# Writing two stages of an attention and expert kernel out in straight code, with the expert tiles inside attention's block

## The chip, the cores and the metric

The kernel runs on one NeuronCore of one Trainium2 chip. The metric is the device time of one execution in microseconds (us), as the median of three runs. One further execution was recorded by the hardware profiler; all rows below are of that one. Engines are named as in the profile: PE (matrix engine; PEld is its weight load), DVE (vector), ACT (scalar), POOL (GpSimd) and SP (whose queue issues most DMAs).

## The reference

The input is x, 8 sequences of 512 tokens with 128 features. All arithmetic is float32.

```
xn = layernorm(x)
s  = attention(xn)         # theta = 0.5 + 0.2 sigmoid(qk) + 0.15 tanh(qk) + 0.1 relu(qk);
                           # softmax(theta) @ v, then the output projection
nf = layernorm(xn) * ln_w + ln_b
e, w = argmax(nf @ router), sigmoid(max(nf @ router))          # one of 8 experts per token
routed = (silu((w nf) @ gate[e]) * ((w nf) @ up[e])) @ down[e]
shared = (silu(nf @ sh_gate) * (nf @ sh_up)) @ sh_down
x  = x + s * silu(xn + routed + shared)
xn = layernorm(x)
x  = x + mamba(xn) * silu(quantised_ffn(xn))                   # state space scan of 16 states
```

## The kernel before, in words

A tile is 128 tokens on 128 partitions; a sequence is 4 tiles (TPB), all tokens are 32 tiles (NT). The kernel is hand written: each engine's program is a list in order, and semaphores join them. It stands in blocks; at a block's end every engine waits for the others.

1. First stage. Moments of all tokens are taken by DVE from `x_all`; then a hardware loop (`Fori`) over the 8 sequences. In each pass DVE makes the normed rows `xn_w` (L307) and twice normed rows `z_w` (L314), and from them `nf_all` (L320, L323). PE turns both (L247, L252), ACT copies them out of PSUM (L213, L217, L220), PE multiplies the turned rows with the value weights (L257) and the router (L263), and DVE writes `vo_all` and `logits` (L328, L333). POOL copies `xn_w` to `res_all` and `xnT_w` to `xnT_all` (L231, L233).
2. Routing. Top, one-hot, counts and the slot of each token, a chain of small DVE instructions (L391 to L434). Tokens are sorted by expert into 40 slot tiles (NT + 8), each of one expert. `guoff` holds each slot tile's expert.
3. Attention, a loop over sequences. Beside it POOL scales rows by their score into `xs_w` (L479) and scatters them to DRAM (`xs_dram`, L486), four indirect DMAs for a sequence.
4. Expert stage, 10 rounds of 4 slot tiles (8 of them in a `Fori`). For tile u: SP loads `xs_t`; PE turns it (`turn_x`, L797); ACT copies it (`x_out`, L864); PE multiplies it with gate and up (`up`, L809); ACT makes a tanh (`tanh`, L869); DVE makes `ha` and `hm` (`hidden`, L888 and L892); PE turns `hm` (`turn_h`, L816); DVE copies it (`h_out`, L898); PE multiplies with down (`dn`, L826); DVE copies the result (`y_out`, L905); SP stores it to `ys_dram` (L778). These are software pipelined over two buffers: in step u PE does `up(u + 1)`, `turn_x(u + 2)`, `dn(u - 1)`, `turn_h(u)`. The expert's number comes into a PE register by `value_load` from `guoff` (`load_expert`, L802, shown by the order as TENSOR_LOAD); the registers don't outlive a pass of the loop, so it is read again:

```
def steps(r, first, last):
    expert.clear()
    load_expert(r, 1)
    if not first:
        load_expert(r, -1)
    for u in range(UN):
        ...                     # up(u + 1), turn_x(u + 2)
        if u == 1:
            load_expert(r, 0)
        ...                     # dn(u - 1), then load_expert(u + 2) for u < 3, turn_h(u)
```

5. Gathering of the expert results, the gate, the second norm. 6. The scan and the quantised network, over half of the time. Stages 5 and 6 are not touched.

Of the kernel before, what the change touches and what calls it, by code (L numbers as in the profile page):

```python
# [5 lines left out]
def attention_moe_mamba_ffn(nc, t, out):  # L6
# [36 lines left out]
    with ctx:  # L43
# [45 lines left out]
        gu = sb("gu", [P, NE, 2 * I])  # L89
        down = sb("down", [P, NE, KI, D])  # L90
# [36 lines left out]
        logits = sb("logits", [P, NT, NE])  # L127
# [14 lines left out]
        with ExitStack() as ph:  # L142
            def sb1(name, shape, dt=fp32):
                return ph.enter_context(nc.sbuf_tensor(name, shape, dt))
            var = sb1("var", [P, NT])
            tmp = sb1("tmp", [P, NT])
            std = sb1("std", [P, NT])
            xn_w = sb1("xn_w", [P, TPB, D])
            z_w = sb1("z_w", [P, TPB, D])
            zw_w = sb1("zw_w", [P, TPB, D])  # L150
            xnT_w = sb1("xnT_w", [P, L])
            nfT_w = sb1("nfT_w", [P, L])
            zeros = sb1("zeros", [P, SLOT_TILES * D // 4])
            bvb = sb1("bvb", [P, P])
            names = {"xn_done": 1, "z_done": 1, "xT_ps": 1, "zT_ps": 1, "xnT_w_done": 1, "nfT_w_done": 1,
                     "vo_ps": 1, "logit_ps": 1, "vo_done": 1, "logit_done": 1, "xnT_copied": 1,
                     "xn_copied": 1, "nfT_copied": 1, "zw": 1, "nf": 1}
            S = {n: sem("p1_" + n) for n in names}
            s_dve = sem("p1_dve_step")
            s_var = sem("p1_var_ready")  # L160
            s_std = sem("p1_std_ready")
            s_zero = sem("p1_zeros_ready")
            s_zd = sem("p1_slots_zeroed")
            s_bvb = sem("p1_bv_broadcast")
            s_wvo = sem("p1_wvo_ps")
            s_wvo_sb = sem("p1_wvo_sb")

            def at(b, n, c=1):
                return (b + 1) * names[n] + c

            block = ph.enter_context(nc.Block())

            @block.sync
            def _(sp):
# [5 lines left out]
                for dst, src in [(WqT[:, :], t["WqT"]), (WkT[:, :], t["WkT"]),  # L180
                                 (shgu[:, 0:I], t["sh_gate"]), (shgu[:, I:2 * I], t["sh_up"]),
                                 (shdown[:, :, :], t["sh_down"].rearrange("(k p) h -> p k h", p=P)),
                                 (gu[:, :, 0:I], t["gate"].rearrange("e h i -> h e i")),
                                 (gu[:, :, I:2 * I], t["up"].rearrange("e h i -> h e i")),
                                 (down[:, :, :, :], t["down"].rearrange("e (k p) h -> p e k h", p=P))]:
# [6 lines left out]
                sp.wait_ge(s_zd, 64)  # L192

            @block.scalar
            def _(act):
# [6 lines left out]
                for dst, src in loads:  # L202
                    act.dma_start(dst, src).then_inc(s_w, 16)
                act.wait_ge(s_var, 1)
                nc.scalar.activation(std[:, :], var[:, :], ACT.Sqrt).then_inc(s_std, 1)
                act.wait_ge(s_var, 2)
                nc.scalar.activation(tmp[:, :], var[:, :], ACT.Sqrt).then_inc(s_std, 1)
                act.wait_ge(s_w, 16 * 12)
                with act.Fori(0, NB) as b:
                    act.wait_ge(S["xT_ps"], at(b, "xT_ps"))  # L210
                    act.wait_ge(S["vo_ps"], at(b, "vo_ps", 0))
                    act.wait_ge(S["xnT_copied"], at(b, "xnT_copied", 0))
                    nc.scalar.activation(xnT_w[:, :], bank[0], ACT.Copy).then_inc(S["xnT_w_done"], 1)  # L213
                    act.wait_ge(S["zT_ps"], at(b, "zT_ps"))
                    act.wait_ge(S["logit_ps"], at(b, "logit_ps", 0))
                    act.wait_ge(S["nfT_copied"], at(b, "nfT_copied", 0))
                    nc.scalar.activation(nfT_w[:, :], bank[1], ACT.Identity, bias=cols[:, 3:4],  # L217
                                         scale=cols[:, 2:3]).then_inc(S["nfT_w_done"], 1)
                    act.wait_ge(S["nfT_w_done"], at(b, "nfT_w_done"))
                    nc.scalar.activation(nfT_all[:, ds(b * L, L)], nfT_w[:, :], ACT.Copy).then_inc(S["nfT_copied"], 1)  # L220

            @block.gpsimd
            def _(pool):
# [3 lines left out]
                for n, per in names.items():  # L227
                    pool.sem_inc(S[n], per)
# [1461 lines left out]
```

## Time and profile before

| what | value |
|---|---|
| median of 3 runs | 908.47 us (906.34 to 909.36) |
| profiled execution: its time | 903.81 us |
| profiled execution: its span, first to last instruction | 901.5 us |
| PE, DVE, ACT, POOL busy, share of the span | 77%, 78%, 52%, 58% |
| first stage and routing | 0 to about 77 us |
| attention | about 77 to 230 us |
| expert stage | about 230 to 342 us |
| gathering, second norm, scan | about 342 to 901.5 us |

A row of the timeline is: start in us, duration in us, engine, line of the kernel, operation, out<-in with shapes, how many instructions were merged, and in brackets how long the engine had been idle before and what released it ("issue": nothing that the profile shows). A row of groups is: line, engine, operation, out<-in, count | busy us, mean ns of one | idle us before them. A row of windows is: stretch, its length, busy us (and instructions) of PE, PEld, DVE, ACT and POOL, granted clock of PE as a share of full speed, busy share of the DMA engines, GB/s.

### The profile page before, as it was taken

To read this page: it belongs to the slowest core of one execution; us is meant where nothing else is said; L and a number is where in the kernel's file an instruction comes from. 1 tells how busy PE (TensorE), PEld (TensorE's weight loads), DVE (VectorE), ACT (ScalarE), POOL (GpSimd) and SP (SyncE) were. 2 spreads that over 40 slices of the span, in tenths; PEclk is the share of its full clock that TensorE was granted. 3 is DMA by queue.
4 is the path that set the end of the run, shared out by engine and by line. 5 is a ranking of instruction groups with operands and counts; after the bars stand their busy time and mean duration, and the time that the engine had idled before them with its cause. 6 is when DMAs were issued, how large, how long until landed. Compare 5 with 4: busy or idle time off the path is not lost. (4 is left out here: it accounts for less than half of the span.)

```text
span 901.5 us, 14653 instructions
## 1 busy us (share of the span) xinstructions
PE 689.7 (77%) x3968; PEld 507.1 (56%) x3969; DVE 702.3 (78%) x1262; ACT 471.3 (52%) x874; POOL 521.4 (58%) x318
## 2 busy tenths in 40 slices
PE   1884999998777772107677988978889798997764
PEld 0771566556344441103346777766777676786763
DVE  5975687877355554881269999998999999999995
ACT  0431666665122221332568586785867869587451
POOL 0213671000000005730478999999899999999993
PEclk9966999999799996556999999999999999999899
DMA  8400110000211111100521142230322204131000
GB/s 233 165 0 15 33 35 12 0 0 0 74 47 50 52 47 35 44 20 1 187 95 54 42 131 71 46 133 25 130 70 65 111 26 150 49 107 71 25 12 12
DMA packets 40046, 55.79 MB, mean 62 GB/s; under 512 B 6584, under 2 KB 29632, under 8 KB 40000
## 3 DMA queue, kind: packets, MB, share of 16 engines
q1 hardware_dynamic: 36224, 50.48, 16.8%
q0 software_dynamic: 2048, 4.20, 1.6%
q10 hardware_dynamic: 1728, 0.57, 0.3%
q8 instruction: 19, 0.31, 0.1%
q14 instruction: 27, 0.22, 0.1%
HBM read 45.54 MB, written 9.70 MB: 61 GB/s over the span
## 5 line engine op out<-in xcount | busy, mean ns | idle before, releaser
L1585 DVE TENSOR_TENSOR_SCAN xnT_all<-psum,nfT_all 128x1024 f32<-128x1024 f32 x128 | 285.6, 2273 | 7.6 <-ACT psum L1435 4.7
L1323 PEld LDWEIGHTS psum<-W_out,xnT_all 128*128 128x128 f32 x2048 | 241.0, 195 | 37.1 <-issue 35.2
L1323 PE MATMUL psum<-W_out,xnT_all 128*128 128x128 f32 x2048 | 243.9, 278 | 16.4 <-DVE acc L1601 16.4
L1435 ACT ACTIVATE psum<-delta,A 128x511 f32<-128x511 f32 x256 | 163.2, 678 | 41.9 <-DVE xnT_all L1585 41.1
L1303 POOL TENSOR_TENSOR nfT_all<-nf_all,du 128x1024 f32<-128x1024 f32 x64 | 149.9, 2367 | 5.1 <-DVE xnT_all L1585 5.1
L1303 POOL TENSOR_TENSOR nfT_all<-attn_all,du 128x1024 f32<-128x1024 f32 x64 | 149.3, 2361 | 1.4 <-POOL du L1280 0.9
L960 POOL COPY pos_w<-pos 128x4 uint32 x8 | 1.6, 198 | 202.7 <-issue 202.5
L1601 DVE SCALAR_TENSOR_TENSOR acc<-psum,Cc,acc 128x128 f32<-128x128 f32 x352 | 96.7, 342 | 7.8 <-PE psum L1323 7.8
L1323 PE MATMUL psum<-vo_all,wgu 128*128 128x512 f32 (+1 forms) x96 | 46.7, 608 | 31.2 <-DVE hff L1621 29.6
L1323 PE MATMUL psum<-vo_all,W_taps 128*128 (+4 forms) x128 | 60.1, 617 | 1.7 <-DVE psum L1568 1.7
L809 PE MATMUL psum<-gu,xT 128*128 x80 | 46.6, 668 | 15.6 <-DVE hm L892 13.5
L864 ACT ACTIVATE xT<-psum 128x128 f32<-128x128 f32 x40 | 11.1, 278 | 80.4 <-PE psum L797 80.4
L981 PE MATMUL psum<-const,xn 128*128 128x128 f32 x32 | 8.3, 434 | 52.7 <-issue 31.5
L1260 POOL TENSOR_TENSOR lg<-lg,rl 128x1024 f32<-128x1024 f32 x8 | 18.8, 2347 | 49.8 <-ACT lg L1501 49.8
L536 PEld LDWEIGHTS psum<-vo_all,PT 128*128 128x128 f32 x256 | 31.8, 195 | 24.1 <-ACT PT L614 16.3
L1323 PEld LDWEIGHTS psum<-vo_all,wgu 128*128 128x128 f32 x96 | 16.3, 189 | 47.6 <-issue 29.4
L964 POOL DMA_INDIRECT moe_w<-ys_dram,pos_w x32 | 33.7, 1053 | 13.9 <-issue 8.9
L1456 ACT ACTIVATE ts<-psum,Cc 128x128 f32<-128x128 f32 x128 | 35.8, 357 | 10.1 <-PE psum L1323 10.1
L486 POOL DMA_INDIRECT xs_dram<-xs_w,pos_w x32 | 32.4, 1012 | 14.7 <-issue 9.9
L1323 PEld LDWEIGHTS psum<-vo_all,W_taps 128*128 128x128 f32 x128 | 24.3, 199 | 27.7 <-issue 25.6
L905 DVE COPY yt<-psum 128x128 f32<-128x128 f32 x40 | 11.7, 292 | 35.5 <-PE psum L826 35.5
L536 PE MATMUL psum<-vo_all,PT 128*128 (+1 forms) x256 | 38.0, 293 | 1.7 <-ACT PT L614 1.4
(202 smaller groups left out, 1261.4 us busy)
## 6 DMA issues: line engine op xcount, KB each, us to landing
attn_all<-bt_dram SPq DMA_DIRECT2D x32, 512.0 KB, 5.4
nf_all<-bt_dram SPq DMA_DIRECT2D x32, 512.0 KB, 3.6
xs_dram<-zeros SPq DMA_DIRECT2D x4, 640.0 KB, 7.3
xs_t<-xs_dram SPq DMA_DIRECT2D x40, 64.0 KB, 1.8
ys_dram<-yt SPq DMA_DIRECT2D x40, 64.0 KB, 1.6
x_all<-in_x_dram SPq DMA_DIRECT2D x8, 256.0 KB, 6.7
out_dram<-ow SPq DMA_DIRECT2D x8, 256.0 KB, 2.3
gu<-in_gate_dram SPq DMA_DIRECT2D x1, 1024.0 KB, 5.9
```

Of the source, the lines that this page charges most:

```text
L486: pool.indirect_dma_start(xs_dram, bass.IndirectOffsetOnAxis(ap=pos_w[:, i, j:j + 1], axis=0), xs_w[:, i, j, :], None).then_inc(s_sc[i], 16)
L536: ins = nc.tensor.matmul(bank[4][:, j * P:(j + 1) * P], PT[:, j % 2, c, :], vo_all[:, ds(b * TPB + c, 1), :], start=(c == 0), stop=(c == T ...
L809: nc.tensor.matmul(bank[2 + u % 2], xT[:, u % 2, :], gu_flat[:, ds(e * (2 * I), 2 * I)], start=True, stop=True).then_inc(S["gu_ps"], 1)
L905: nc.vector.tensor_copy(yt[:, u % UN, :], bank[6 + u % 2][:, 0:D]).then_inc(S["y"], 1)
L964: pool.indirect_dma_start(moe_w[:, i, j, :], None, ys_dram, bass.IndirectOffsetOnAxis(ap=pos_w[:, i, j:j + 1], axis=0)).then_inc(s_moe[i], 16)
L1260: nc.gpsimd.tensor_tensor(lg[:, :, :], lg[:, :, :], rl[:, :, :], ALU.add).then_inc(S["sp"], 1)
L1303: nc.gpsimd.tensor_tensor(dbx[:, i % R, :, :], B_pair(q), du[:, p, h:h + 1, :].to_broadcast([P, 2, L]), ALU.mult)\
L1323: return nc.tensor.matmul(o, l, r, start=start, stop=stop)
L1435: ins = nc.scalar.activation(dA[:, i % RA, k, 1:L], delta[:, p, h, 1:L], ACT.Exp, scale=A[:, h, 2 * q + k:2 * q + k + 1])
L1456: ins = nc.scalar.activation(ts[:, i, j, :], bank[Gb[n % 2]][:, j * P:(j + 1) * P], ACT.Copy, scale=Cc[:, p, j, n:n + 1])
L1585: nc.vector.tensor_tensor_scan(hring[:, i % R, :, :].rearrange("p n l -> p (n l)"), dA[:, i % RA, :, :].rearrange("p n l -> p (n l)"), dbx ...
L1601: nc.vector.scalar_tensor_tensor(acc[:, p, j, :], bank[Gb[m % 2]][:, j * P:(j + 1) * P], Cc[:, p, j, m:m + 1], acc[:, p, j, :] if i else s ...
```

## The change

First stage and routing become one block and are written out over the 8 sequences, with no loop. The norms are written straight to `res_all` and the turned rows to `xnT_all` and `nfT_all`, so the copies by POOL and by ACT (L220) are gone. `nf_all` is no longer made on DVE: PE turns `nfT_all` back (`turn_back`), and ACT writes it multiplied by the score (`scaled`); attention's POOL multiplies no more. The moments' chain is shorter, and the first norm starts before the second variance is known. Logits stay in PSUM, and DVE takes each sequence's top from there.

The scatters read `pos` and `nf_all` directly, and POOL waits after each four. The expert stage stands in attention's block: no block end between them, its buffers lie over `xnT_all`, and SP loads the first four slot tiles once the last keys have been multiplied. It is written out over the 40 tiles. Gate, up and down lie in one tensor `gud`, with one offset for an expert (its number times `WE`), read once for each tile. `y_out` has moved from DVE to ACT.

```
-            names = {"xn_done": 1, "z_done": 1, ...
-                with act.Fori(0, NB) as b:
...
-                    nc.scalar.activation(nfT_all[:, ds(b * L, L)], nfT_w[:, :], ACT.Copy).then_inc(S["nfT_copied"], 1)
-                with pool.Fori(0, NB) as b:
...
-                    nc.gpsimd.tensor_copy(res_all[:, ds(b * TPB, TPB), :], xn_w[:, :, :]).then_inc(S["xn_copied"], 1)
...
-                    nc.gpsimd.tensor_copy(xnT_all[:, ds(b * L, L)], xnT_w[:, :]).then_inc(S["xnT_copied"], 1)
+                def turn_back(b):
+                    if b >= 2:
+                        pe.wait_ge(S["xs"], b + 1 - 2)
+                    for i in tiles(b):
+                        ins = nc.tensor.transpose(bank[bN[b % 2]][:, cols4(i)], nfT_all[:, i * P:(i + 1) * P], ident)
+                    ins.then_inc(S["nf_ps"], 1)
...
+                for b in range(NB + 1):
+                    if b < NB:
+                        turn_x(b)
+                        turn_z(b)
+                    if b == 0:
+                        pe.wait_ge(s_wvo_sb, 1)
+                        pe.wait_ge(s_vob, 1)
+                        continue
+                    values(b - 1)
+                    route(b - 1)
+                    turn_back(b - 1)
...
+                def scaled(b):
+                    act.wait_ge(S["score"], b + 1)
+                    act.wait_ge(S["nf_ps"], b + 1)
+                    for i in tiles(b):
+                        ins = nc.scalar.activation(nf_all[:, i, :], bank[bN[b % 2]][:, cols4(i)], ACT.Copy,
+                                                   scale=score[:, i:i + 1])
+                    ins.then_inc(S["xs"], 1)
...
+                for b in range(NB):
+                    turned_x(b)
+                    turned_z(b)
+                    if b >= 1:
+                        half_scores(b - 1)
+                    if b >= 2:
+                        scaled(b - 2)
...
+                for b in range(1, NB):
                     norms(b)
-                    values_logits(b - 1)
-                values_logits(NB - 1)
+                    norms2(b)
+                    if b >= 2:
+                        values(b - 2)
+                        tops(b - 2)
+                    if b >= 3:
+                        scores(b - 3)
...
-                        nc.gpsimd.tensor_tensor(xs_w[:, i, :, :], nf_all[:, ds((b2 * 2 + i) * TPB, TPB), :],
...
+                for i in range(NT):
+                    pool.indirect_dma_start(xs_dram, bass.IndirectOffsetOnAxis(ap=pos[:, i:i + 1], axis=0),
+                                            nf_all[:, i, :], None).then_inc(s_sc, 16)
+                    if i % TPB == TPB - 1:
+                        pool.wait_ge(s_sc, (i + 1) * 16)
...
+                sp.wait_ge(S["k_ps"], at(NB - 1, "k_ps", 1))
+                sp.wait_ge(s_sc, NT * 16)
+                for u in range(UN):
+                    sp.dma_start(xs_t[:, u, :], slots(xs_dram, u)).then_inc(s_in[u], 16)
...
+                for u in range(SLOT_TILES):
+                    if u + UN < SLOT_TILES:
+                        sp.wait_ge(E["xT_ps"], u + 1)
+                        sp.dma_start(xs_t[:, u % UN, :], slots(xs_dram, u + UN)).then_inc(s_in[u % UN], 16)
+                    sp.wait_ge(E["y"], u + 1)
+                    sp.dma_start(slots(ys_dram, u), yt[:, u % UN, :]).then_inc(s_out[u % UN], 16)
...
+                def load_expert(u):
+                    expert[u] = pe.value_load(guoff[0:1, u:u + 1], min_val=0, max_val=(NE - 1) * WE)
...
+                for u in range(SLOT_TILES):
+                    if u + 1 < SLOT_TILES:
+                        up(u + 1)
+                    if u + 2 < SLOT_TILES:
+                        load_expert(u + 2)
+                    if u + 2 < SLOT_TILES:
+                        turn_x(u + 2)
+                    if u:
+                        dn(u - 1)
+                    turn_h(u)
+                dn(SLOT_TILES - 1)
...
+                for u in range(SLOT_TILES):
+                    tanh(u)
+                    if u + 2 < SLOT_TILES:
+                        x_out(u + 2)
+                    if u:
+                        y_out(u - 1)
+                y_out(SLOT_TILES - 1)
...
-                        if not (first and u == 0):
-                            y_out(r, u - 1)
...
+                for u in range(SLOT_TILES):
+                    hidden(u)
+                    h_out(u)
```

How the instructions stand. First PE in the expert stage before, from the start of a pass of the loop to the second tile's `turn_h` (the ISA and REGISTER_ALU rows set registers or semaphores):

```order
L802 TENSOR_LOAD guoff
L802 ISA x3
L802 TENSOR_LOAD guoff
L802 ISA x2
L806 ISA
L809 ISA
L809 MATMUL psum<-gu,xT 128x512
L795 REGISTER_ALU
L796 REGISTER_ALU
L797 MATMUL psum<-const,xs_t 128x128
L822 REGISTER_ALU
L826 ISA
```

and PE there now, one tile in full (the buffers bear the name of `xnT_all`, over which they lie):

```order
L664 ISA
L664 MATMUL psum<-gud,xnT_all 128x512
L655 TENSOR_LOAD guoff
L655 ISA x2
L650 MATMUL psum<-const,xnT_all 128x128
L688 ISA
L688 MATMUL psum<-gud,xnT_all 128x128
L688 ISA
L688 MATMUL psum<-gud,xnT_all 128x128
L676 MATMUL psum<-const,xnT_all 128x128 x2
```

Two reads of the expert in a row stood ahead of a pass's first `up` (and three or four more stood in the pass, 6 for 4 tiles); now one read stands behind each `up`. On ACT in the expert stage, before:

```order
L869 ACTIVATE th<-psum 128x256
L862 REGISTER_ALU
L864 ACTIVATE xT<-psum 128x128
L867 REGISTER_ALU
L869 ACTIVATE th<-psum 128x256
```

and now (L786 is `tanh`, L780 `x_out`, L793 `y_out`):

```order
L786 ACTIVATE xnT_all<-psum 128x256
L780 ACTIVATE xnT_all<-psum 128x128
L793 ACTIVATE xnT_all<-psum 128x128
L786 ACTIVATE xnT_all<-psum 128x256
L780 ACTIVATE xnT_all<-psum 128x128
```

Each tanh now stands behind the copy of an earlier tile's result. On DVE at the start of the first stage, behind the moments, now (L356 is `norms`, L365 `norms2`):

```order
L391 TENSOR_TENSOR dif<-stats 128x32
L392 TENSOR_TENSOR mean_r<-stats 128x32
L393 TENSOR_TENSOR sumsq<-stats 128x32
L394 TENSOR_SCALAR mean_r<-mean_r 128x32
L395 TENSOR_TENSOR dif<-dif 128x32
L396 SCALAR_TENSOR_TENSOR sumsq<-dif,sumsq 128x32
L399 RECIPROCAL rstd<-std 128x32
L356 TENSOR_SCALAR res_all<-x_all,mean_r,rstd 128x128 x4
L401 TENSOR_TENSOR tmp<-rstd 128x32
```

Before, 21 small instructions stood there ahead of the first norm (L134 to L301); now 7 do.

## Rows read from the trace of the kernel before

**Rows 1.** Windows: attention, expert stage.

```profile
77.00:229.70 152.70, 139.50 (x672) 87.06 (x672) 110.37 (x192) 90.35 (x184) 42.51 (x48) 0.96 0.05 14
240.00:339.90 99.90, 77.58 (x345) 44.00 (x344) 56.30 (x155) 21.33 (x74) 0.00 (x0) 1.00 0.18 51
```

**Rows 2.** Timeline, PE, expert stage: one pass of the loop.

```profile
278.13 1.12 PE L809 MATMUL psum<-gu,xT 128*128 x2 [1.71 <-DVE hm L892]
279.20 0.61 PE L826 MATMUL psum<-down,hT 128*128 x4
280.07 1.12 PE L809 MATMUL psum<-gu,xT 128*128 x2
282.62 1.12 PE L809 MATMUL psum<-gu,xT 128*128 x2
...
288.57 1.12 PE L809 MATMUL psum<-gu,xT 128*128 x2 [1.72 <-DVE hm L892]
```

**Rows 3.** Timeline, PE: attention's last product, first expert tiles.

```profile
226.84 2.07 PE L536 MATMUL psum<-vo_all,PT 128*128 128x128 f32 x8 [0.69 <-ACT PT L614]
...
232.42 0.47 PE L797 MATMUL psum<-const,xs_t 128*128 128x128 f32 x1 [0.17 <-DMA xs_t<-xs_dram]
233.52 3.78 PE L809 MATMUL psum<-gu,xT 128*128 x4 [0.63 <-ACT xT L864]
...
238.11 1.35 PE L809 MATMUL psum<-gu,xT 128*128 x2 [0.17 <-issue]
```

**Rows 4.** Groups of DVE's instructions in the expert stage (one of three alike).

```profile
L892 DVE SCALAR_TENSOR_TENSOR hm<-ha,psum 128x256 f32<-128x256 f32 x38 | 16.0, 421 | 2.1
```

**Rows 5.** Timeline, expert stage: ACT's tanh, SP's store and next load.

```profile
284.06 0.38 ACT L869 ACTIVATE th<-psum 128x256 f32<-128x256 f32 x1
...
282.56 0.35 SPq L778 DMA_DIRECT2D ys_dram<-yt  x1
283.16 0.34 SPq L776 DMA_DIRECT2D xs_t<-xs_dram  x1
```

**Rows 6.** Instructions of tile xs_t: from issue to landing.

```profile
DMA to landing us min/median/max: 1.7/1.8/3.0
```

**Rows 7.** Timeline: the last tile's up, and the next block's first instruction.

```profile
334.48 1.12 PE L809 MATMUL psum<-gu,xT 128*128 x2
...
341.99 0.18 DVE L1016 TENSOR_SCALAR A<-A 128x32 f32<-128x32 f32 x1 [2.11 <-PEq L726]
```

**Rows 8.** Timeline, DVE, start of the first stage.

```profile
13.90 0.21 DVE L134 TENSOR_TENSOR mean_r<-stats 128x32 f32<-128x32 f32 x1
...
20.61 1.12 DVE L307 TENSOR_SCALAR xn_w<-x_all,mean_r,rstd 128x128 f32<-128x128 f32 x4 [0.23 <-DVE vobias L301]
```

**Rows 9.** Windows, first stage: one pass at half, one at full clock.

```profile
46.79:52.14 5.35, 5.35 (x25) 4.98 (x25) 5.09 (x14) 2.01 (x3) 1.27 (x2) 0.50 0.00 0
37.05:40.67 3.62, 2.94 (x26) 2.73 (x26) 3.46 (x10) 1.80 (x3) 0.62 (x1) 1.00 0.00 0
```

**Rows 10.** Timeline, PE, first stage: transposes, then a slow spell's ends, last product.

```profile
28.31 1.06 PE L252 MATMUL psum<-const,z_w 128*128 128x128 f32 x4
...
44.95 2.05 PE L257 MATMUL psum<-Wvo,xnT_w 128*128 128x128 f32 x8 [1.88 <-DVE vo_all L328]
...
57.50 1.05 PE L263 MATMUL psum<-router,nfT_w 128*128 128x8 f32 x8
...
61.11 0.96 PE L263 MATMUL psum<-router,nfT_w 128*128 128x8 f32 x8
```

**Rows 11.** Timeline, first stage: DVE's norms beside POOL's copy.

```profile
25.01 1.10 DVE L307 TENSOR_SCALAR xn_w<-x_all,mean_r,rstd 128x128 f32 x4
26.04 1.53 DVE L314 TENSOR_SCALAR z_w<-x_all,mean_r,rstd 128x128 f32 x4
26.29 0.69 POOL L231 COPY res_all<-xn_w 128x512 f32 x1 [1.74 <-DVE xn_w L307]
```

**Rows 12.** Groups of instructions, 25 to 61 us: DVE's vo_all.

```profile
L328 DVE TENSOR_TENSOR vo_all<-psum,vobias 128x512 f32 x7 | 4.8, 683 | 0.0
```

More of the change, by code:

```diff
@@ L395, in _ @@
+                for b in (NB - 2, NB - 1):
+                    values(b)
+                    tops(b)
+                    scores(b - 1)
+                dve.wait_ge(S["top"], NB)
+                link(nc.vector.tensor_tensor(eq[:, :, :], logit, top[:, :, None].to_broadcast([P, NT, NE]), ALU.is_equal))
+                scores(NB - 1)
                 link(nc.vector.tensor_tensor(eq[:, :, :], eq[:, :, :],
@@ new lines, in up, with turn_h @@
+                def up(u):
+                    pe.wait_ge(E["xT"], u + 1)
+                    if u >= 2:
+                        pe.wait_ge(E["hm"], u - 1)
+                    else:
+                        pe.wait_ge(S["pT_sb"], at(NB - 1, "pT_sb", TPB - 1 + u))
+                    alone(pe)
+                    nc.tensor.matmul(bank[2 + u % 2], xT[:, u % 2, :], gud_flat[:, ds(expert[u], 2 * I)],
+                                     start=True, stop=True).then_inc(E["gu_ps"], 1)
+                def turn_h(u):
+                    pe.wait_ge(E["hm"], u + 1)
+                    if u >= 2:
+                        pe.wait_ge(E["hT"], u - 1)
+                    elif u == 1:
+                        pe.wait_ge(S["shh"], at(NB - 1, "shh", KI))
+                    else:
+                        pe.wait_ge(S["attn"], at(NB - 1, "attn", 1))
+                    for k in range(KI):
+                        ins = nc.tensor.transpose(bank[4 + u % 2][:, k * P:(k + 1) * P],
+                                                  hm[:, u % 2, k * P:(k + 1) * P], ident)
+                    ins.then_inc(E["hT_ps"], 1)
@@ new lines, in dn @@
+                def dn(u):
+                    pe.wait_ge(E["hT"], u + 1)
+                    if u >= 2:
+                        pe.wait_ge(E["y"], u - 1)
+                    elif u == 1:
+                        pe.wait_ge(S["res"], at(NB - 1, "res", 1))
+                    alone(pe)
+                    for k in range(KI):
+                        ins = nc.tensor.matmul(bank[6 + u % 2][:, 0:D], hT[:, u % 2, k, :],
+                                               gud_flat[:, ds(expert[u] + (2 * I + k * D), D)],
+                                               start=(k == 0), stop=(k == KI - 1))
+                    ins.then_inc(E["y_ps"], 1)
+                    del expert[u]
@@ L907, in steps @@
-                def steps(r, first):
-                    for u in range(UN):
-                        hidden(r, u)
-                        if not (first and u == 0):
-                            y_out(r, u - 1)
-                        h_out(r, u)
-                steps(0, True)
-                with dve.Fori(1, ROUNDS) as r:
-                    steps(r, False)
-                y_out(ROUNDS - 1, UN - 1)
+                        .then_inc(E["hT"], 1)
+                for u in range(SLOT_TILES):
+                    hidden(u)
+                    h_out(u)
```

588 lines of the change are left out of this document (241 added, 347 removed).

## The prediction

> **What bounds the kernel now.** I read the windows first. Attention fills PE for 139.5 of 152.7 us; the expert stage fills it for only 77.6 of 99.9 us, at granted clock 1.00 (2.4 GHz), with DVE at 56 [rows 1]. So the expert stage has some 22 us in which no engine is the bound, and the timeline says where they are. A pass of 4 slot tiles takes 288.57 - 278.13 = 10.44 us. Its first tile takes 280.07 - 278.13 = 1.94 us and its second 2.55; third and fourth together take 5.95 [rows 2]. The 1.94 is PE back to back: `dn` starts 1.07 after `up`, and the next `up` 0.87 later. At the end of a pass PE is idle for 1.72 us; the row names DVE's `hm`, but the `hm` for which that `up` waits is that of two tiles earlier, long done, so this is PE's own sequencer: the branch and two reads of `guoff`. What one read costs shows at the stage's start: between the second transpose (232.42) and the first `up` (233.52) stands one read, and the copy it needs ends earlier: about 1.0 us [rows 3]. Two reads in a row make the 1.72; the other tiles above 1.94 hold a read where PE has little queued.
>
> The first stage has two regimes. In a slow pass the granted clock is 0.50 (1.2 GHz) and PE is busy 5.35 of 5.35 us: PE is the bound. In a fast one (1.00) PE needs 2.94 of 3.62 us, DVE 3.46 [rows 9]; there DVE is the bound. One slow spell lasted from 44.95, after 1.88 us of idle PE, to 57.50 [rows 10].
>
> **The change, expert stage.** (1) Start. Attention's last PE product ends at 226.84 + 2.07 = 228.91 [rows 3]. Two reads stand behind it in PE's program; its sequencer comes to them soon after 226.84, so they end near 229.1. The slot tiles were loaded long ago. Transpose (0.47) and ACT's copy (about 0.3) put the first `up` at 229.85 instead of 233.52. The first two tiles run at the lower level as before: from first to third `up` 238.11 - 233.52 = 4.59 [rows 3], so the third is at 234.45.
> (2) The tile. One read a tile, behind `up`, whose two passes keep PE busy for 0.96 of the 1.12 us [rows 2]. The sequencer comes to the read once `turn_h` and `up` are issued, at the latest when `up` starts; then a 1.0 us read ends about 0.05 late, and if it runs ahead nothing is lost. PE's sum stays 1.94. Three other loops close over a tile and must fit in it. DVE: `h_out`, `ha`, `hm` at 0.42 each [rows 4] and `turn_h` 0.4 with hand-overs: 1.75. ACT: the tanh of u + 1 now stands behind `y_out` of u - 1, which waits for `dn`; from one `dn`'s end: copy 0.3, tanh 0.38 [rows 5], `ha`, `hm` 0.85, then PE's `turn_h`, `up`, transpose and `dn` 2.1 and hand-overs of 0.1: 3.7 us for two tiles, 1.86 each. SP: the load of u + 4 is issued 0.60 after a store [rows 5] and lands 1.8 later [rows 6]; with store hand-over 0.2, transpose, `dn` and `y_out` 1.1 it makes 3.7 for two tiles, 1.85 each. All lie 0.1 to 0.2 below 1.94: PE stays the bound, but with little room, and the landing's maximum is 3.0 [rows 6]. I take 2.0 us a tile. Bounds: 1.94 (PE's own sum), 2.55 (the second tile as before, nothing gained in it).
> (3) From the third `up` to the fortieth are 37 steps: 37 x 2.0 = 74 us, to 308.45. The tail from the last `up` to the next block, 341.99 - 334.48 = 7.5 [rows 7], holds the same instructions: 316.0 instead of 342.0. Gain 26.0 us (28.2 at 1.94; 5.6 at 2.55).
>
> **The change, first stage.** (4) Start. Moments end at 13.90, the first norm starts at 20.61 [rows 8]. Now 6 small instructions, a square root on ACT and a reciprocal stand between: at the before's pace of about 0.2 each, 0.3 and 0.35, the first norm is at 15.5. The second variance is worked out behind it (1.4 us more), so DVE ends norms of sequence 0 at 19.2 and of sequence 1 at 21.4; PE turns the latter until 22.4.
> (5) PE's work. Removed: nothing. Added: `turn_back`, 4 transposes, 1.06 less an overlap of 0.2 at the lower level [rows 10], 0.45 at the higher. So a pass costs PE 5.35 + 0.87 = 6.2 us at half and 2.94 + 0.45 = 3.4 at full clock [rows 9].
> (6) DVE's work. Two norms, `vo_all`, top, score. The first norm takes 1.10; the second took 1.53 with POOL's copy beside it [rows 11]; with no copy I take 1.10. With `vo_all` 0.68 [rows 12] and two small ones of 0.2, and gaps, 3.45. So a fast pass takes 3.5. If the 0.43 were the second norm's own, it would be 3.9, and five or six fast passes would cost 2 us more.
> The Trainium skill (SBUF — State Buffer, "Who interferes with whom") says that such a DVE copy or scalar form and a GpSimd instruction exclude each other from a shared pair of ports for a whole instruction. By that rule the 0.43 us goes away with POOL's copy, which is what the row suggests too.
> (7) How long PE stays at the lower level. The one spell with both ends in rows lasted 12.5 us, PE all but unbroken [rows 10]. From 21.4, where PE's work becomes unbroken, that is 33.9. Then: values to `turn_back` of the first pass end at 26.8, one pass at 6.2 to 33.0, the third nearly all at full clock (3.9) to 36.9, four passes of 3.5 to 50.9, last values and logits 1.8: 52.7. Before, the last logits' product ends at 61.11 + 0.96 = 62.07. Gain 9.4 us. Bounds: lower level throughout, 26.8 + 6 x 6.2 + 3.5 = 67.5, a loss of 5.4; full clock after 5 us, as the expert stage's first spell (233.52 to 238.11 [rows 3]), 49.6, a gain of 12.5.
> The Trainium skill (TensorE: Matmul & The Clock Gate, "What's actually happening") says that the clock follows how busy PE is, and rises once it has been busy without a break for a short while. By that rule the 12.5 us gain would stand in the sum in place of 9.4, 3 us faster; the spell of 12.5 us shows that these small matmuls raise it later.
>
> **The rest, at nothing.** POOL's multiply and copies leave attention; PE's 139.5 of 152.7 us covers them, and uncovered they are worth under 1 us. Scatters start no later and are followed by 80 us of attention without POOL. The split weight load has the same bytes. Routing keeps its chain, less one instruction of 0.4. ACT's added work in the first stage (`scaled`) replaces L220.
>
> **Sum.** 26.0 + 9.4 = 35.4 us. The profiled execution took 903.8 (span 901.5), 4.7 below the median of the runs shown, 908.5: own time 868.4, median 873.
>
> **Rivals.**
> A. The forecast, 864 to 880: chance 0.60.
> B. The tile stays at 2.2 to 2.55 because one of the near loops (ACT's tanh behind `y_out`, or SP's load) becomes the bound. For it: margins of 0.1 to 0.2. Against: each has been summed below 1.94. At 2.35 the gain shrinks by 37 x 0.35 = 13: 886. Chance 0.17.
> C. First stage at the lower level throughout. For it: PE fell back to it at 44.95. Against: there PE had idled 1.88 us waiting for `vo_all`, and a pass now leaves 0.1. Loss 5.4 for the gain 9.4: 888. Chance 0.13.
> D. The reads and the branch weren't the cost, and the tile keeps its mean of (334.48 - 233.52) / 39 = 2.59: gain from (1), 3.7, and (7) alone: 895. Against: the four-tile pattern, whose plain tile is at 1.94. Chance 0.05.
> E. The other side. ACT's queue ties each tile to the one before: tanh waits for `y_out`, it for `dn`, and `up`, tanh, `ha`, `hm`, `turn_h`, `h_out`, `dn` follow one another: 1.12 + 0.38 + 3 x 0.42 + 0.43 + 0.61 + 0.3, seven hand-overs of 0.1: 4.8 us a tile, 2.2 x 39 = 86 above before, less 13: 981. It decides once a tile takes over 2.59 + 13.1 / 37 = 2.95. Against: `y_out` waits for the tile two back, not one. Chance 0.03. Fetching the written-out code would end on this side too, from the same 2.95. It and all else: 0.02.
>
> **How the numbers follow.** Likeliest 873. Chances below 864 and above 890 are to make 0.2 together: D, E, the rest and the upper part of C and B lie above, a little of A's lower end below. Range 862 to 890. A difference within 0.3% (2.7 us) can hardly be told from none. Faster: A to D, 0.95; slower 0.04; same 0.01.
>
> **What would show it.** Right: in the expert stage every `up` 1.95 to 2.05 us after the last, no idle of PE above 0.3, first `up` within 1.2 us of attention's last product; the first norm near 15.5, the last logits near 53, the clock at 1.00 from about 34. Wrong: `turn_x` released by the DMA in most tiles (SP's loop), `turn_h` released by `hm` with DVE idle on the tanh (ACT's loop), granted clock 0.50 in the first stage's middle.

## The result, and the profile after

The changed kernel took 856.18 us in the median of 4 runs (854.45 to 858.41), the kernel before 907.4 beside it (4 runs). The ratio is 0.9447, with a 95% interval of 0.9413 to 0.9481; in a second comparison of 6 and 11 runs it was 0.9464 (0.9437 to 0.9491). The forecast of 873 was 17 us too slow, and 856 lies outside its range.

The profiled execution took 857.77 us (span 856.0): 46.0 less than the profiled 903.81 of before, where the sum forecast 35.4; by the medians it is 51.2 (907.40 - 856.18). These are the windows of after, for the first stage's fast part, attention, and the expert stage without its ends (columns as in [rows 1]).

```profile
25.13:46.58 21.45, 21.45 (x199) 21.45 (x199) 17.34 (x61) 15.27 (x44) 0.00 (x0) 1.00 0.31 127
60.48:209.97 149.49, 138.44 (x672) 86.13 (x672) 107.75 (x191) 89.98 (x184) 32.25 (x32) 0.97 0.07 21
220.00:282.00 62.00, 59.63 (x288) 35.82 (x286) 38.22 (x96) 26.07 (x95) 0.00 (x0) 1.00 0.24 68
```

PE now fills 21.45 of 21.45 us of the first stage and 59.6 of 62.0 of the expert stage, against 77.6 of 99.9 [rows 1]. Next the timeline of PE after: hand-over from attention to the experts, one plain tile late in the stage, the fortieth `up`, and DVE's first instruction of the next block.

```profile
208.81 1.16 PE L600 MATMUL psum<-vo_all,PT 128*128 128x128 f32 x8 [0.69 <-ACT PT L745]
210.45 0.43 PE L650 MATMUL psum<-const,xnT_all 128*128 128x128 f32 x2 [0.49 <-issue]
211.36 1.98 PE L664 MATMUL psum<-gud,xnT_all 128*128 x4 [0.48 <-ACT xnT_all L780]
...
214.13 1.08 PE L664 MATMUL psum<-gud,xnT_all 128*128 x2
...
276.65 1.04 PE L664 MATMUL psum<-gud,xnT_all 128*128 x2
277.53 0.27 PE L650 MATMUL psum<-const,xnT_all 128*128 128x128 f32 x1
277.70 0.71 PE L688 MATMUL psum<-gud,xnT_all 128*128 x4
278.24 0.38 PE L676 MATMUL psum<-const,xnT_all 128*128 128x128 f32 x2
278.46 1.06 PE L664 MATMUL psum<-gud,xnT_all 128*128 x2
...
285.75 1.12 PE L664 MATMUL psum<-gud,xnT_all 128*128 x2
...
293.21 0.18 DVE L1006 TENSOR_SCALAR A<-A 128x32 f32<-128x32 f32 x1 [3.38 <-PEq L467]
```

Attention's last product ends at 208.81 + 1.16 = 209.97, and the first `up` follows at 211.36. The third is at 214.13, the fortieth at 285.75, the next block at 293.21. A plain tile takes 278.46 - 276.65 = 1.81 us. The first stage, after:

```profile
14.54 0.19 DVE L396 SCALAR_TENSOR_TENSOR sumsq<-dif,sumsq 128x32 f32<-128x32 f32 x1
14.81 1.28 ACT L326 ACT_TABLE_LOAD   x1 [14.81 <-DVE sumsq L396]
16.11 0.32 ACT L326 ACTIVATE std<-sumsq,eps 128x32 f32<-128x32 f32 x1
16.46 0.35 DVE L399 RECIPROCAL rstd<-std 128x32 f32<-128x32 f32 x1 [1.73 <-ACT std L326]
16.85 1.12 DVE L356 TENSOR_SCALAR res_all<-x_all,mean_r,rstd 128x128 f32<-128x128 f32 x4
...
22.52 1.12 PE L242 MATMUL psum<-const,z_w 128*128 128x128 f32 x4
23.64 1.67 PE L250 MATMUL psum<-Wvo,xnT_all 128*128 128x128 f32 x7
25.13 0.97 PE L259 MATMUL psum<-router,nfT_all 128*128 128x8 f32 x8
...
26.87 0.60 PE L242 MATMUL psum<-const,z_w 128*128 128x128 f32 x4
27.30 1.06 PE L250 MATMUL psum<-Wvo,xnT_all 128*128 128x128 f32 x8
28.20 0.96 PE L259 MATMUL psum<-router,nfT_all 128*128 128x8 f32 x8
```

The clock level is read from the four transposes: 1.12 us at 22.52 (the lower), 0.60 at 26.87 (the higher). The column of the granted clock is no safe sign here: in the window from 22.52 to 23.40 it already stands at 1.00. From 25.13 the level is the higher one, to the end of the stage. Passes take 28.20 - 25.13 = 3.07, the later ones 3.05.

Where the gain came from, stretch by stretch (profiled executions; the spans differ by 901.5 - 856.0 = 45.5 us):

| stretch | before | after | gain | forecast |
|---|---|---|---|---|
| start to the last logits' product | 62.07 | 46.58 | 15.5 | 9.4 |
| routing, to attention's first product | 14.88 | 13.90 | 1.0 | 0 |
| attention, to its last product's end | 151.96 | 149.49 | 2.5 | 0 |
| to the first `up` | 4.61 | 1.39 | 3.2 | 3.7 |
| first to third `up` | 4.59 | 2.77 | 1.8 | 0 |
| third to fortieth `up` | 96.37 | 71.62 | 24.8 | 22.4 |
| fortieth `up` to the next block | 7.51 | 7.46 | 0 | 0 |
| the untouched rest | 559.5 | 562.8 | -3.3 | 0 |

### The profile page after: what moved, and what is told of

It reads as the page before. It is cut to its first block and busy times, and to the rows that moved or that the text cites. A ratio compares the mean times of both kernels' runs of the same rounds, so it can differ in the third digit from the quotient of the medians.

```text
span 856.0 us, 13812 instructions
## 1 busy us (share of the span) xinstructions
PE 679.6 (79%) x4000; PEld 502.5 (59%) x4000; DVE 672.5 (79%) x1203; ACT 484.5 (57%) x946; POOL 501.5 (59%) x289
## 5 line engine op out<-in xcount | busy, mean ns | idle before, releaser
L1313 PEld LDWEIGHTS psum<-W_out,xnT_all 128*128 128x128 f32 x2048 | 244.1, 197 | 40.0 <-issue 38.0
L1313 PE MATMUL psum<-W_out,xnT_all 128*128 128x128 f32 x2048 | 246.5, 280 | 17.2 <-DVE acc L1591 17.2
L551 POOL DMA_INDIRECT xs_dram<-nf_all,pos x32 | 32.3, 1008 | 66.7 <-issue 55.9
L1313 PE MATMUL psum<-vo_all,wgu 128*128 128x512 f32 (+1 forms) x96 | 49.6, 642 | 26.5 <-DVE hff L1611 24.9
L664 PE MATMUL psum<-gud,xnT_all 128*128 x80 | 43.4, 626 | 0.5 <-ACT xnT_all L780 0.5
L901 DVE COPY xnT_all<-psum 128x256 f32<-128x256 f32 x40 | 17.0, 425 | 27.4 <-PE psum L676 27.4
L971 PEld LDWEIGHTS psum<-const,xn 128*128 128x128 f32 x32 | 5.7, 216 | 54.5 <-issue 53.5
```

Source lines behind the costliest of these rows:

```text
L551: pool.indirect_dma_start(xs_dram, bass.IndirectOffsetOnAxis(ap=pos[:, i:i + 1], axis=0), nf_all[:, i, :], None).then_inc(s_sc, 16)
L664: nc.tensor.matmul(bank[2 + u % 2], xT[:, u % 2, :], gud_flat[:, ds(expert[u], 2 * I)], start=True, stop=True).then_inc(E["gu_ps"], 1)
L901: nc.vector.tensor_copy(hT[:, u % 2, :, :], bank[4 + u % 2][:, 0:KI * P].rearrange("p (k s) -> p k s", s=P))\
L1313: return nc.tensor.matmul(o, l, r, start=start, stop=stop)
```

## The experiments

**The two halves.** e1_first_stage has the first stage, routing and scatters of after with the expert stage of before; e2_experts is the reverse. Their diffs are the halves of the change's diff.

> The first stage and routing of after (with nf_all scaled on ACT and the scatters reading it directly), all else as before: expert stage in its own block, in its loop. The profile of after puts attention's first product at 60.5 us, of before at 77.0: 16.5 us. Theory 1 (the two halves of the change add up): 16 to 18 us faster than before, about 890, and the expert stage keeps its 10.44 us pass. Theory 2 (part of the gain exists only when both halves are there): under 14 us faster.

> The expert stage of after inside attention's block, written out, one offset a tile; first stage, routing and POOL's multiply and scatters as before. Theory 1 (the halves add up): the rest of the 51 us, 31 to 35 us faster, about 874, first stage ending near 77 us, tiles at 1.83 us where the load is in time. Theory 2 (the higher clock at the hand-over comes from something in the first half): only about 29 us faster, the first two tiles at the lower level as before (4.6 us from first to third up).

e1 took 885.11 us, ratio 0.9771 (0.9724 to 0.9818): 20.7 us. e2 took 877.18, ratio 0.9696 (0.9640 to 0.9752): 27.5 us. Neither lies in the range written for it: e1 gained more than 16 to 18 us, e2 less than 31 to 35. Their sum, 48.2, is the whole 50 (907.4 x 0.0553) within the intervals, which are 4 to 5 us wide on either side of each. In e1's profile the last logits end at 46.67, so e1 has the whole of the first stage's gain; in e2's the next block starts at 311.93, 30.1 earlier than before [rows 7], though its first stage ended 2.2 later than before's. From first to third `up` e2 took 2.78 us and from third to fortieth 71.75, as the changed kernel does, so theory 2 fails there. Nothing larger than these intervals hangs on the two together.

**Do the reads hold PE?** e3_before_const is the kernel before with the two reads at a pass's start replaced by constants (some tiles then use a wrong expert's weights). e4_two_reads is the changed kernel with a second read.

```diff
e3  -                    load_expert(r, 1)
e3  +                    expert[1] = 1
e3  -                        load_expert(r, -1)
e3  +                        expert[-1] = 0
e4                           load_expert(u + 2)
e4  +                        load_expert(u + 2)
```

> The kernel before, with the two reads of guoff at the start of each pass of the expert loop replaced by constants (experts 1 and 0 for those products, so the output is another). Theory 1, the prediction's (the two reads, 1.0 us each, make PE's 1.72 us of idle at a pass's start): a pass takes 8.7 to 8.9 us instead of 10.44, the stage 14 us less. Theory 2 (the branch and fetching the code behind it make the idle): a pass stays at 10.2 to 10.4.

> The changed kernel with the expert's number read twice for every tile instead of once. Theory 1 (a read of guoff holds PE's sequencer for about 1.0 us; one a tile hides behind the up and down products, two in a row don't): the plain tile goes from 1.83 to 2.7 to 2.9 us, up(2) to up(39) from 71.6 to 100 to 107 us, and the kernel is 28 to 35 us slower than the changed one. Rival (the sequencer runs ahead of PE and reads are free wherever they stand, so that what the loop cost was its branch): the tile stays within 1.83 to 1.95 and the time within 2 us.

The timeline of PE in e3 (`up` alone), one pass:

```profile
278.13 1.12 PE L809 MATMUL psum<-gu,xT 128*128 x2
280.02 1.10 PE L809 MATMUL psum<-gu,xT 128*128 128x512 f32 x2
282.30 1.12 PE L809 MATMUL psum<-gu,xT 128*128 x2
285.14 1.12 PE L809 MATMUL psum<-gu,xT 128*128 x2
287.04 1.12 PE L809 MATMUL psum<-gu,xT 128*128 x2
```

The pass falls from 10.44 [rows 2] to 287.04 - 278.13 = 8.91 us, though the branch is still there: the two reads ahead of a pass, with the register work on what they read, cost 1.53, 0.77 each. Third to fortieth `up` took 82.95 us instead of 96.37, near the 14 us expected. In e4:

```profile
285.09 1.02 PE L664 MATMUL psum<-gud,xnT_all 128*128 x2
286.34 0.30 PE L650 MATMUL psum<-const,xnT_all 128*128 128x128 f32 x1 [0.23 <-issue]
286.63 0.71 PE L688 MATMUL psum<-gud,xnT_all 128*128 x4
287.18 0.38 PE L676 MATMUL psum<-const,xnT_all 128*128 128x128 f32 x2
287.40 1.02 PE L664 MATMUL psum<-gud,xnT_all 128*128 x2
```

The transpose behind the reads starts 1.25 after `up` instead of 0.88, and the tile takes 2.31. Third to fortieth `up` took 87.0 us (71.6 with one read), the kernel 873.6 us in one run. That is 0.42 a tile, less than half of what was expected, but far from nothing: one read hides behind `up`, a second no longer does. e4 reads 2 times a tile and takes 2.35 on average; before read 1.5 times a tile and took 2.61. So the number of reads alone doesn't set the tile; where they stand seems to count for more, though before's tile also holds the loop and separate offsets for `down`.

**What makes some tiles long?** e6_eight_ahead loads slot tiles 8 ahead instead of 4; e9_y_on_dve puts `y_out` back on DVE, between `hidden` and `h_out`.

```diff
e6  -            xs_t = over[:, 0:UN * D].rearrange("p (u d) -> p u d", d=D)
e6  +            UL = 8
e6  +            xs_t = over[:, 3072:3072 + UL * D].rearrange("p (u d) -> p u d", d=D)
...
e6  -                    if u + UN < SLOT_TILES:
e6  +                    if u + UL < SLOT_TILES:
e9                       hidden(u)
e9  +                    if u:
e9  +                        y_out(u - 1)
e9                       h_out(u)
```

> The changed kernel with slot tiles loaded 8 ahead instead of 4 (the buffers lie elsewhere over xnT_all). Theory 1 (the tiles above 1.83 us wait for a slot tile that was requested only after the store of a result, and landed late): no transpose waits for the load, every tile 1.83 to 1.95, up(2) to up(39) 68 to 70 us, 2 to 4 us less than the changed kernel. Rival (PE's queue hides the late loads, other waits make the long tiles): up(2) to up(39) within 0.7 us of 71.6.

> The changed kernel with the copy of a tile's result (y_out) back on DVE, between the product of the gated tile and the copy of its turned form. Theory 1 (with the reads gone, the tile stands close to DVE's chain, so the move to ACT was needed to get below 1.94): DVE's chain gets 0.3 longer, the tile 1.95 to 2.25 us, up(2) to up(39) 76 to 83 us, the kernel 4 to 11 us slower than the changed one. Rival (DVE has room): up(2) to up(39) stays at 70 to 73 us.

The waits of the changed kernel in its expert stage name the loads (us in total, times, longest):

```profile
PEld psum L650 <- DMA xnT_all<-xs_dram: 19.9, 31, 1.8
...
PE psum L650 <- DMA xnT_all<-xs_dram: 2.3, 4, 1.0
```

Most of the 19.9 is the idle time of the weight load beside a busy PE. In PE's own idle time it is 2.3 us in 4 tiles, such as this one, where SP took 1.10 us to issue a load, and the transpose at 222.77 came late:

```profile
220.21 1.10 SPq L540 DMA_DIRECT2D xnT_all<-xs_dram  x1
...
222.77 0.14 PEld L650 LDWEIGHTS psum<-const,xnT_all 128*128 128x128 f32 x1 [0.94 <-DMA xnT_all<-xs_dram]
```

In e6 the DMA is in no row of the waits. Third to fortieth `up` took 284.62 - 216.63 = 67.99 us, 3.6 less, 1.84 a tile: the first theory. One issue on SP took even 1.55 us there, and no wait of PE followed. The one run took 849.7 us, but only 3.6 of its distance to 856 belongs to this (the rest varies, below). In e9 the same stretch took 71.71 us and the kernel 856.4: no change, the rival. With loads 4 ahead DVE had the room, and the move to ACT gained nothing.

**The clock level in the first stage.** e5_no_skew takes the shift by one sequence out of PE's program, so that each pass waits for its own copies.

```diff
-                for b in range(NB + 1):
-                    if b < NB:
-                        turn_x(b)
-                        turn_z(b)
+                for b in range(NB):
+                    turn_x(b)
+                    turn_z(b)
...
-                    values(b - 1)
-                    route(b - 1)
-                    turn_back(b - 1)
+                    values(b)
+                    route(b)
+                    turn_back(b)
```

> After, with PE's order in the first stage as before: values, routing product and turning back of a sequence right behind its transposes, not one sequence later, so PE has to wait for ACT's copies in each pass. Theory 1 (short breaks in PE's work keep it at the lower level): the slow passes last several times as long as after's, the last logits come at 55 to 65 us instead of 46.6. Theory 2 (the level rises with the amount of work, the added transposes above all): full clock from about 25 us as in after, a pass 3.3 to 3.6 us instead of 3.05, the last logits at 49 to 51.

It took 862.2 us, last logits at 52.35, outside both ranges. PE waited 0.25 us in each pass, the level rose at about 29.9 and stayed. So small gaps don't bring it down, and my first reading fell; the late rise is no sign of the gaps, as it came as late in e6, e11 and e12, which have none there. In the old form's traces the level alternates: before, a slow spell begins at 44.95 behind a wait of 1.88 us [rows 10]; in e2 one begins behind this:

```profile
30.24 2.05 PE L258 MATMUL psum<-Wvo,xnT_w 128*128 128x128 f32 x8 [2.00 <-DVE vo_all L329]
```

The three traces of the old form (before, e2, e3) hold five such falls, behind waits of 1.77 to 2.00 us. Each time the first product behind the wait was already slow, and each spell lasted 12.5 us. To make such waits in the changed kernel I added DVE instructions of 128x512 whose result nobody reads: n in every sequence, m in the fifth (the two lines on S["extra"] stand only in the runs with n above 0).

```diff
                     ins.then_inc(S["z"], 1)
+                    if b:
+                        dve.wait_ge(S["extra"], b)
+                    for k in range(m if b == 4 else n):
+                        ins = nc.vector.tensor_tensor(extra[:, k, :, :], x_all[:, b * TPB:(b + 1) * TPB, :],
+                                                      rows[:, 1:2, :].to_broadcast([P, TPB, D]), ALU.mult)
+                    ins.then_inc(S["extra"], 1)
```

> The changed kernel with two more DVE instructions of 128x512 for each sequence in the first stage, whose result nobody reads, so that DVE bounds its pass at the higher clock level, as in the kernel before. Theory 1 (the clock level falls back in the first stage where PE waits for DVE at the higher level): the pass gets about 3.8 us with 0.7 us of PE idle, the level falls at least once after it rose (four transposes at 1.1 again), and the last logits' product ends at 56 us or later. Rival (these idles don't matter; the level stays up once it is up): four transposes stay at 0.62 from about 26 us on, and the last logits end at 50 to 54 us.

> The changed kernel with five DVE instructions of 128x512 added in one sequence of the first stage alone (the fifth), whose result nobody reads. They make PE wait once for about 2 us while the level is the higher one. Theory 3 (before, each fall followed one wait of 1.9 to 2.0 us; the run with 0.7 us of idle in every pass did not fall): after this wait four transposes take about 1.1 us again for some passes, and the last logits end at 51 to 56 us. Rival (idle time isn't what brings the level down, but something that grows with the loop or with POOL's work): they stay at 0.62, and the last logits end 1.5 to 3 us later than in the changed kernel, at 48 to 50 us.

> As e11_one_long with three such instructions instead of five: one wait of PE of about 1 us. Theory 3 allows both, and this run says on which side such a wait lies: no fall, last logits 0.5 to 1.5 us later than in the changed kernel; or a fall, 50 us or later. The rival expects no fall.

> As e11_one_long, which made PE wait 1.69 us once and kept the higher level, with six such instructions instead of five: one wait of about 2.3 us. Theory 3 (each fall before followed one wait of 1.88 to 2.00 us; 1.69 was just too short): four transposes take about 1.1 us again behind the wait, for 3 us or more, and the last logits end 3 us or more behind where the wait alone would put them. Rival (one wait doesn't bring the level down in this form, whatever its length): they stay at 0.60 to 0.64, and the last logits end at 49 to 52 us, by when the level first rose.

> As e13_idle_a with eight such instructions: one wait of about 3.6 us. Theory 3: a fall behind the wait, as in the other run. Rival: none.

> As e10_dve_work (two added DVE instructions in every sequence, PE idle for 0.74 us in every pass, no fall), with four instead of two in the fifth sequence, so that one wait there lasts about 2.0 us. Theory 4 (the falls before came from a wait of 1.9 to 2.0 us on top of a pass in which PE had idled already; alone 0.74 in each pass, 1.69 or 2.29 once don't suffice): four transposes take about 1.1 us again behind that wait. Rival (only a wait near 3.5 us does it): they stay at 0.60 to 0.64.

> As e15_both_waits with five in the fifth sequence: one wait of about 2.7 us among waits of 0.74 us. Theory 4: a fall, as there. Rival: none, or one here alone.

| run | n, m | PE's waits at the higher level, us | level falls | last logits end | time, one run |
|---|---|---|---|---|---|
| e10 | 2, 2 | 0.7 in every pass | no | 53.07 | 858.4 |
| e12 | 0, 3 | 0.48 once | no | 50.24 | 862.6 |
| e11 | 0, 5 | 1.69 once | no | 51.04 | 858.5 |
| e13 | 0, 6 | 2.29 once | no | 48.43 | 856.1 |
| e14 | 0, 8 | 3.50 once | yes | 55.64 | 864.1 |
| e15 | 2, 4 | 0.7 in every pass, 1.94 once | yes | 53.76 | 857.9 |
| e16 | 2, 5 | 0.7 in every pass, 2.54 once | yes | 55.64 | 862.6 |

One wait of 2.29 us in an otherwise busy stage leaves the level up; here is the timeline of PE in e13, with the transposes behind the wait at 0.60:

```profile
35.18 1.13 PE L251 MATMUL psum<-Wvo,xnT_all 128*128 128x128 f32 x8 [2.29 <-DVE vo_all L375]
36.15 0.96 PE L260 MATMUL psum<-router,nfT_all 128*128 128x8 f32 x8
36.96 0.63 PE L268 MATMUL psum<-const,nfT_all 128*128 128x128 f32 x4
37.43 0.60 PE L235 MATMUL psum<-const,res_all 128*128 128x128 f32 x4
```

A shorter wait, 1.94 us, among passes that idle 0.7 us each was followed by a fall, in e15:

```profile
37.60 1.13 PE L251 MATMUL psum<-Wvo,xnT_all 128*128 128x128 f32 x8 [1.94 <-DVE vo_all L378]
38.57 0.96 PE L260 MATMUL psum<-router,nfT_all 128*128 128x8 f32 x8
39.38 0.86 PE L268 MATMUL psum<-const,nfT_all 128*128 128x128 f32 x4
40.03 1.06 PE L235 MATMUL psum<-const,res_all 128*128 128x128 f32 x4
40.89 1.06 PE L243 MATMUL psum<-const,z_w 128*128 128x128 f32 x4
41.74 1.70 PE L251 MATMUL psum<-Wvo,xnT_all 128*128 128x128 f32 x8
43.28 0.96 PE L260 MATMUL psum<-router,nfT_all 128*128 128x8 f32 x8
```

So theory 3, that one wait of about 2 us brings it down, fell in e13, and the wait's length alone doesn't decide. Theory 4, that what PE idled around the wait counts too, was formed after e14 and was right in both of its runs, and the pass of before had both, 0.69 and 0.30 us of idle PE ahead of the 1.88. But each run is one execution, and the first fall of e2 had only 0.18 us ahead of its 2.00 in the same pass.

There is a rival that these runs don't rule out: that the same waits sometimes end in a fall and sometimes don't. At the end of attention PE waits 1.03, 0.69 and 0.69 us in the changed kernel and in e13 alike. The changed kernel's last eight products took 1.16 us (208.81, above), those of e13:

```profile
207.57 1.19 PE L604 MATMUL psum<-vo_all,PT 128*128 128x128 f32 x8 [0.69 <-ACT PT L749]
210.30 2.07 PE L604 MATMUL psum<-vo_all,PT 128*128 128x128 f32 x8 [0.69 <-ACT PT L749]
```

The times written for the last logits were missed in three runs. In e11 and e12 they came late, as the level first rose at about 30 instead of 25 us; in e13 they came at 48.43, ahead of the 49 to 52 of its rival, which held.

**A version that is better.** e7_both has e6's loads, and one more line for ACT at the first stage's start, which makes it load the table of the square root early:

```diff
+                nc.scalar.activation(half[:, 0:1], eps[:, 0:1], ACT.Sqrt)
```

> The changed kernel with slot tiles loaded 8 ahead, and with a square root of one column on ACT at the first stage's start, so that its table is loaded before the variance is ready. Theory 1 (late loads cost 3.7 us in the expert stage, the table load 1.3 us ahead of the first norm): the first norm starts at 15.4 to 15.7 us instead of 16.85, up(2) to up(39) takes 68.0 us, and the median is 4 to 5.5 us below that of the changed kernel beside it. Rival (the start's gain is eaten because the clock level rises at the same time anyway): the first norm is earlier but the first stage ends within 0.5 us of the other's, and the median is 3 to 4 us lower.

> The changed kernel once more, beside e7_both on one chip: 853 to 859 us, ratio to the kernel before 0.942 to 0.948. A second profile of it shows how far its parts vary: last logits 45.5 to 50 us, up(2) to up(39) 71 to 72.5 us.

```profile
7.32 1.28 ACT L325 ACT_TABLE_LOAD   x1 [7.32 <-issue]
8.61 0.20 ACT L325 ACTIVATE half<-eps 128x1 f32<-128x1 f32 x1
...
15.80 1.12 DVE L357 TENSOR_SCALAR res_all<-x_all,mean_r,rstd 128x128 f32<-128x128 f32 x4
```

e7 took 852.48 us (6 runs), ratio 0.9390 (0.9360 to 0.9421); the changed kernel beside it 857.94. That is 5.5 us less, at the upper end of what was expected. Third to fortieth `up` took 67.97 us against 71.74; from the end of the moments' chain to the first norm it is 1.35 us shorter (15.80 - 14.83 against 17.43 - 15.12). The first norm's 15.80 missed its 15.4 to 15.7 because the chain itself ended 0.3 us later than in the changed kernel's first profile, behind the loads of x. The last logits end 0.9 earlier than in a_again, where the first norm is 1.6 earlier: part of the gain at the start was kept.

## Why the prediction was wrong

Two terms of the sum failed above all: the time at the lower clock level in the first stage (step 7: to last until 33.9 us, it ended at 25.1) and the length of a fast pass there (steps 5 and 6: 3.5 us, measured 3.05). The profiled executions differ by 10.6 us more than the sum: 6.1 from the first stage, 3.8 from the expert stage, 3.5 from what was put at nothing, -3.3 from the untouched rest, and 0.5 between time and span. The other 6.3 of the 17 come from the last line of the sum. It took over from before that a median lies 4.7 above the profiled execution; the changed kernel's median lies 1.6 below it.

1. **The expert stage, steps 1 to 3: right, a little too careful.** The reads were a large part of the cost (e3, e4, and item 2), the tile came down to PE's own work, PE stayed the bound, and a straight sum gave 26.0 where 29.8 came. Terms: the tile was put at 2.0 for the near loops and took 71.62 / 37 = 1.94. The plain tile is even 1.81 to 1.83, less than the 1.94 that I took for PE's own sum. The near loop that bit was SP's, in some tiles (rival B in small: 3.6 us, e6). The lower level for the first two tiles, 1.8 us, did not come in this execution. Attention handed over within 1.4 us instead of 4.6, but that isn't shown to be the reason: in e11 and e14 the hand-over took 1.4 us as well, and the first two tiles were slow again, 4.3 us from first to third `up`.
2. **A read's size, step 1: over-sized in part.** The 1.0 us was read at one place of the kernel before [rows 3] and was not tried there; ahead of a pass e3 gives 0.77. Of the 10.44 - 4 x 1.83 = 3.1 us that a pass lost, e3 accounts for half. How the other half divides between the reads inside the pass and the loop was not tried.
3. **The start, step 4: 1.35 us too early.** The sum left out ACT's table load (1.28 us). Before, it was done long ahead of the square root:

```profile
7.51 1.28 ACT L205 ACT_TABLE_LOAD   x1 [7.51 <-issue]
```

In the new order it stands behind the wait for the variance (14.81, above). e7 gives it back.
4. **The passes, steps 5 and 6: too long by 0.45.** A fast pass took 3.05, not 3.5, and over six passes that is 2.7 us. DVE's work is as expected: the second norm takes 1.12 without POOL's copy (1.53 with it [rows 11]), with which the rule that I named of the Trainium skill (SBUF — State Buffer, "Who interferes with whom") agrees. Its sum of 3.45 a pass was too high: I had put its instructions end to end with gaps, where in the rows neighbours overlap by some 0.1. From 32 to 39 us, where passes are full, DVE is busy for 6.70 of 7.00 us; so it fits into 3.05 with little room, and e10 shows the same (4.03 a pass with 1.3 added). PE bounds the pass, and its sum of 3.4 was high too: the window with 2.94 us [rows 9] held 26 matmuls where a pass had 24, and 28 of them now take 3.05.
5. **The clock level, step 7: the step that failed.** I took a spell of 12.5 us, which stood behind a fall, for the time to the first rise. All five spells behind a fall in the old form's traces lasted 12.5 us, but the first rise is another matter. In the straight form it came 3 to 5 us after unbroken work began in eleven executions, and 8.5 to 9.7 us after it in four (e5, e6, e11, e12); in the old form it came after about 4 us in e2 and e3, and after 15 us in the kernel before. The difference between the two groups is 3 us in the last logits (46.6 against 49.9 in e6). In the profiled execution the early rise was worth 4.5 us against the sum: 1.4 in the first values' pass (3.0 instead of 4.4), 2.7 in the second (the 6.2 against a fast 3.5) and 0.4 in the third. With 2.7 from item 4, less 1.0 for the later start, that is the 6.1 us of this stage. The old form also paid for its falls: before, the 12.5 us of one spell held 2.3 passes of 5.35 instead of 3.62 us [rows 9, 10], about 4 us lost. That was in the 62.07 from which the gain was reckoned. In e14, where PE bounds the pass, the fall cost 4.9: from the first product behind the wait to the last logits' end it took 55.64 - 37.46 = 18.18 us, in e13 48.43 - 35.18 = 13.25. By the durations the level stayed low for about 10 us there, and for about 3.4 us in e15 and e16. In e15 and e16, where DVE bounds the pass, the fall cost nothing that I can see: the last logits end where e10's plus the added instructions would. The rule of the Trainium skill (TensorE: Matmul & The Clock Gate, "What's actually happening") that I had set aside was nearer: with it the sum gave 12.5 us of gain, the trace 15.5. It agrees with the eleven early rises; a short while doesn't fit the four late ones, nor the spells of 12.5 us. Rival C, the lower level throughout, showed in no run.
6. **"The rest, at nothing": 3.5 us in sum.** Attention gained 2.5. From its first product to the first transposes of scores it took 11.93 us instead of 12.48, and its last 9.3 us shrank by 1.4, as before's level had fallen there (2.07 us for the last eight products against 1.16); that POOL's missing multiply has a share in it was not tried. Routing gained 1.0. The untouched rest took 3.3 more, for another reason: it took 555.8 to 563.8 us over all these traces. These are the windows of the same stretch in the changed kernel and in e6, both with nothing changed there:

```profile
500.00:700.00 200.00, 184.71 (x1219) 147.70 (x1218) 190.22 (x262) 138.02 (x242) 192.19 (x94) 0.97 0.21 73
```

```profile
500.00:700.00 200.00, 183.39 (x1225) 146.67 (x1225) 191.73 (x269) 141.28 (x246) 194.73 (x96) 1.00 0.23 79
```

Where this window's clock was 0.97 or 0.98, the rest took 562.0 to 563.8 us, where it was 0.99 or 1.00, 555.8 to 559.5 (e2: 561.4). Which of the two an execution gets isn't explained.

## What to carry to other kernels

Straightening a stage is worth what its engine idles, and in this stage that could be read as a pattern: find the plain pass among the slow ones, and ask what stands on the sequencer ahead of the others. Here a register read from memory cost PE 0.77 us for each of two ahead of a pass and 0.42 us for a second one behind `up`, and the one behind `up` cost nothing to be seen; so place it there.

Where a stage is at two clock levels, don't take the length of a spell behind a fall for the time to the first rise; the two differed here. Look in the trace for the wait ahead of each fall, and whether the change takes it away.

When a first activation is moved behind a wait, its table load moves with it; a dummy one ahead of the wait kept it hidden in e7.

## What the runs showed that I had not expected

- The length of one wait doesn't decide whether the level falls: 2.29 us once left it up, 1.94 among waits of 0.7 did not. The idle time around it fits all runs of the changed kernel, but the end of attention shows a fall and no fall behind the same waits.
- The same code of the first stage took about 3 us more or less by when the level first rose (24 to 25, or about 31 us), with PE's unbroken work beginning at 20.5 to 21.3 us in all of them.
- One issue of a load on SP took 1.10 us instead of 0.43; with loads 4 ahead PE waited for DMA, with 8 ahead it did not, though one issue took 1.55.
